# Moving small VectorE operations of the state-space front to GpSimd and ScalarE, and regrouping TensorE's sums and transposes

## The chip, the core and the metric

The kernel runs on one core of a Trainium2 chip, as one program. The metric is the device time of that core in microseconds. The engines work through queues of their own and meet only in semaphores: TensorE (PE) multiplies, VectorE (DVE), ScalarE (ACT) and GpSimd (POOL) work element by element, SyncE (SP) issues the DMAs. In the profile a line such as L1766 is a line of the kernel before.

## What is computed

x is 64 x 64 x 256 (64 sequences of 64 steps, width 256). Two attention layers are added to it, then two state-space layers. The change touches only the state-space layers, and of these only the part ahead of the scan, called the front here:

```python
xr, gate = jnp.split(x @ W_in.T, 2, axis=-1)
xr = xr + t_emb[:, None, :]
xc = silu(causal depthwise conv of width 4 over xr + b_conv)
mu = xc.mean(-1, keepdims=True)
var = xc.var(-1, keepdims=True)
xn = (xc - mu) / jnp.sqrt(var + 1e-05) * ln_g + ln_b
Bm, Cm, dt = jnp.split(xn @ W_xproj.T, 3, axis=-1)
dt = jnp.tanh(dt @ W_dt.T + b_dt) * 0.01
A = -jnp.tanh(A_log)
Ad = 1.0 + dt * A
Bd = Bm * jnp.minimum(jnp.linalg.norm(xn, axis=-1, keepdims=True), 1.0)
# scan over time: h = clip(h * Ad + Bd * xn, -10, 10); y = C h
```

## The kernel before

The 64 sequences are cut into 8 groups of 8, so a group has 512 tokens (columns) and the inner width 512 lies in 4 blocks of 128 partitions. A layer runs a front over the groups, a scan in two passes of four groups, and an output part. The program is written for each engine by hand: every engine has a `body(it, ...)` that lists its work for one group, and the order in that list is the order in its queue. The loop over the groups 0 to 5 and a body for group 6 (`ahead` false) come first; group 7 is spread over the first steps of the scan (`last_group`). Ahead of body 0 a few lines start group 0.

A body of the front works on two groups at once: the second half of the front of group `it`, and the first half of group `it + 1`. The steps, with the lines of the program:

- TensorE makes the X part (`x_in_proj`, L1177) and the gate part (`gate_in`, `gate_half`, L1177 and L1337) into PSUM banks 0 to 3. VectorE adds the condition (`embed`, L1762), ScalarE makes the first tap of the convolution (`tap`, L796), VectorE the other three (`conv`, L1766, twelve of 512 columns), ScalarE the SiLU (`conv_silu`, L801).
- The mean: TensorE sums with columns of ones (`mean`, L1344, tile 128*32). To spread it over all partitions exactly, the row is split in three bf16 parts: `high` (L893), `remain` (VectorE, `mean_rest`, L1899), `middle` (GpSimd, `mean_middle`, L611), `rows3` (VectorE, `mean_rows`, L1904), and TensorE spreads it (`spread_out`, L1350). VectorE subtracts it (`centred`, L1895, four), ScalarE squares (L909, four), TensorE sums the squares (`variance`, L1344).
- The standard deviation: ScalarE takes Ln and Exp (`log_std`, L913 and L915), VectorE makes a Newton step in three operations (`root`, L1607, L1609, L1611) and has `zr`. Then the same split: `high` on GpSimd (L601), `remain` (L1909), `middle` on GpSimd (L606), `rows3` (L1914), spread, and VectorE multiplies (`gained`, L1924, four), ScalarE adds the bias (`shifted`, L919) and squares again (`squared`, L923).
- The small projections: TensorE has `project_part` (L1369, tile 128*32), the product for dt (`decay`, L1382), the norm sums (`norm`, L1344). ScalarE has `decay_tanh`, VectorE `decay` (`am`, L1935), GpSimd 1/`am` in four operations (`over_decay`, L589 to L596, `rc`). VectorE bounds the squared norm (`norm_bound`, L1929), ScalarE takes Ln and Exp (`log_norm`, L940 and L942), VectorE makes a Newton step and a product (`inverse_norm`), multiplies with 1/`am` (`over_decay`, L1950, `mr`), makes `rB` (`scaled_b`, L1955) and the product carried to the next step, `eC` (`carried`, L1959). TensorE folds both (`fold_b`, L1391 and L1393), VectorE splits the result into three bf16 parts (`split_b`, L1970 to L1976, `tvp`).
- The turns: TensorE transposes the normed x (`turned_x`, L1386, tile 128*128), and it is split in three bf16 parts: `xh` on ScalarE (`high_part`, L947), the rest `xr1` on VectorE (`rest`, L1964), `xmi` on ScalarE (`middle_part`, L951), `xlo` on GpSimd (`last_parts`, L584). SP stores them (`store_parts`), and stores `sg` (`store_gate`), the normed x (`store_x`), C and the decay (`store_decay`) and the parts of B (`store_b`, six DMAs) for each group.

ScalarE holds one of two tables at a time, and loads another with `silu_set` and `logarithm_set` (L708, L704), once each in a body.

## Time and profile before

| | |
|---|---|
| median of 3 runs | 1785.19 us (1783.34 to 1785.89) |
| the profiled execution | 1782.5 us, its span 1780.7 us |
| TensorE busy | 1680.3 us, 94% of the span |
| VectorE busy | 1609.2 us, 90% |
| ScalarE busy | 1306.8 us, 73% |
| GpSimd busy | 685.2 us, 38% |
| VectorE, `conv` (L1766) | 192 of 749 ns, 134.6 us |
| TensorE, X and gate products (L1177) | 456 records of 606 ns, 213.6 us |
| GpSimd, `Uw` of the scan (L627) | 256 of 1345 ns, 335.5 us |

The page gives a single profiled execution. Its 40 slices show the attention until slice 12, then for each layer the front in about four slices, the scan, and the output. A timeline lists one engine's instructions in order of time, with neighbours of one line merged (x4 means four); "idle before" is the time in which the engine had nothing to do, and behind the arrow stands who released it. TensorE's matmuls are pipelined, so the differences of their starts say more than their durations. A 512-column product in float32 has two records.

### The profile page before, as it was taken

The page shows a single profiled execution, that of the slowest core. Times are in us where ns is not written, and L with a number is a line of the kernel's source. Part 1 is how long each engine was busy: PE and PEld are TensorE (multiplying, and loading weights), DVE is VectorE, ACT ScalarE, POOL GpSimd, SP SyncE. Part 2 cuts the span into 40 slices and gives each one's busy share as a digit, 9 for nine tenths or more (in the row PEclk, how much of TensorE's full clock was granted, in tenths as well). Part 3 has the DMA queues.
Part 4 walks back from the last instruction along what each step waited for, and adds up shares of the span by engine and source line. Part 5 has one row for each costly group of instructions (what it writes and reads, how often), then busy time and mean ns, then how long its engine had stood idle before and what let it go on. Part 6 is the DMA issues. An engine that isn't in the chain of part 4 may idle for free. (4 is left out here: it accounts for less than half of the span.)

```text
span 1780.7 us, 43798 instructions
## 1 busy us (share of the span) xinstructions
PE 1680.3 (94%) x14852; PEld 750.7 (42%) x14852; DVE 1609.2 (90%) x2492; ACT 1306.8 (73%) x2213; POOL 685.2 (38%) x702
## 2 busy tenths in 40 slices
PE   7999999999999999789999999999998899999998
PEld 3555555555554555332222224445553322222244
DVE  5899999899877999989999997679999999999975
ACT  5655566565646999889999992079998899999910
POOL 0233233323332223557676550012235576756400
PEclk9999999999999999899999999999998999999999
DMA  4000000000002444544545667524446445456678
GB/s 163 2 1 0 1 1 32 2 1 0 1 1 87 172 152 165 192 146 138 183 149 190 226 187 236 190 87 172 174 145 204 141 150 178 145 195 195 188 232 272
DMA packets 126456, 226.85 MB, mean 127 GB/s; under 512 B 35620, under 2 KB 61220, under 8 KB 117540
## 3 DMA queue, kind: packets, MB, share of 16 engines
q1 hardware_dynamic: 125912, 223.51, 38.1%
q10 hardware_dynamic: 432, 1.84, 0.3%
q8 instruction: 71, 1.16, 0.3%
q14 instruction: 41, 0.34, 0.1%
HBM read 141.95 MB, written 83.36 MB: 127 GB/s over the span
## 5 line engine op out<-in xcount | busy, mean ns | idle before, releaser
L1062 ACT ACTIVATE R<-q,Ast 128x512 f32<-128x512 f32 x1016 | 632.9, 709 | 34.4 <-DVE q L2084 32.1
L2084 DVE SCALAR_TENSOR_TENSOR q<-R,PS 128x512 f32<-128x512 f32 x1008 | 610.6, 680 | 9.4 <-ACT R L1062 6.4
L627 POOL TENSOR_TENSOR Uw<-Ub,rowmask 96x512 bf16<-96x512 bf16 x256 | 335.5, 1345 | 144.0 <-PE PS L1509 131.8
L1509 PE MATMUL PS<-xq,Uw 97*128 97x512 bf16 x1024 | 326.6, 391 | 46.8 <-DVE q L2084 37.4
L1526 PE MATMUL PS<-q,Wy 128*32 128x512 f32 x2016 | 280.1, 611 | 0.4 <-DVE q L2084 0.4
L1509 PEld LDWEIGHTS PS<-xq,Uw 97*128 97x128 bf16 x1024 | 84.6, 97 | 363.5 <-DVE q L2084 271.1
L1177 PE MATMUL PS<-X,Win 128*128 (+1 forms) x456 | 213.6, 606 | 0.1
L1078 PE MATMUL PS<-xn,Wl 128*128 128x512 f32 x384 | 188.0, 614 | 0.7 <-DVE xn L1648 0.7
L548 POOL TENSOR_TENSOR ex<-ex,rs 128x1024 f32<-128x1024 f32 x32 | 77.5, 2423 | 203.2 <-DVE rs L1671 203.2
L1766 DVE SCALAR_TENSOR_TENSOR acc<-xp,Wc,acc 128x512 f32<-128x512 f32 x192 | 134.6, 749 | 2.6 <-DVE eC L1888 0.2
L1177 PEld LDWEIGHTS PS<-X,Win 128*128 128x128 f32 x456 | 82.6, 191 | 92.1 <-issue 91.3
L1575 PE MATMUL PS<-yg,Wo 128*128 128x512 f32 x256 | 113.9, 599 | 0.0
L1529 PE MATMUL PS<-xq,By 96*32 96x512 bf16 x1024 | 110.7, 385 | 0.0
L796 ACT ACTIVATE acc<-xp,Ch,Wc 128x512 f32<-128x512 f32 x64 | 51.9, 815 | 74.7 <-DVE xp L1762 74.5
L772 ACT ACTIVATE vTd<-PS 128x1024 f32<-128x1024 f32 x32 | 32.8, 1025 | 94.4 <-PE PS L1078 94.4
L780 ACT ACTIVATE pT<-PS 128x512 f32<-128x512 f32 x128 | 69.3, 593 | 43.4 <-PE PS L1155 43.2
L1078 PEld LDWEIGHTS PS<-xn,Wl 128*128 128x128 f32 x384 | 66.1, 191 | 56.2 <-issue 51.8
L1658 DVE TENSOR_REDUCE mx<-PS 128x32 f32<-128x2048 f32 x32 | 73.2, 2286 | 17.9 <-PE PS L1139 17.8
L541 POOL TENSOR_TENSOR vsc<-vTd,vs_t 128x1024 f32<-128x1024 f32 x16 | 38.3, 2396 | 110.3 <-ACT vTd L772 110.3
L1668 DVE TENSOR_REDUCE sm<-ex 128x32 f32<-128x2048 f32 x32 | 72.9, 2279 | 6.7 <-ACT ex L784 6.7
L1155 PE MATMUL PS<-ident,ex 128*128 128x128 f32 x512 | 69.3, 277 | 6.5 <-DVE ex L1675 4.5
L2122 DVE SCALAR_TENSOR_TENSOR yf<-xnp,Dsk,PS 128x512 f32<-128x512 f32 x64 | 43.6, 743 | 33.2 <-DMA sgp<-sg_d 30.6
(183 smaller groups left out, 2630.9 us busy)
## 6 DMA issues: line engine op xcount, KB each, us to landing
xq<-xpart_d SPq DMA_DIRECT2D x384, 192.0 KB
sg_d<-sg SPq DMA_DIRECT2D x16, 1024.0 KB, 5.2
xn_d<-z SPq DMA_DIRECT2D x16, 1024.0 KB, 3.9
y_d<-ys SPq DMA_DIRECT2D x64, 256.0 KB, 3.9
xnp<-xn_d SPq DMA_DIRECT2D x16, 1024.0 KB, 8.2
sgp<-sg_d SPq DMA_DIRECT2D x16, 1024.0 KB, 11.7
xpart_d<-xh SPq DMA_DIRECT2D x16, 512.0 KB, 2.9
xpart_d<-xmi SPq DMA_DIRECT2D x16, 512.0 KB, 3.7
```

The source lines that it names most:

```text
L548: pl.tensor_tensor(late_half(ex, r), late_half(ex, r), rs[:, r, :].rearrange("p (j e) -> p j e", j=4)[:, :, 4:8] .unsqueeze(3).broadcast_t ...
L627: pl.tensor_tensor(Uw[0:XROWS, h, w, :, :, :], Ub[0:XROWS, w, 0:N, ds(s0, CH)].rearrange("p n t -> p t n").unsqueeze(2).broadcast_to([XROW ...
L1062: act.activation((end if end and (h, t) == (1, CH - 1) else R)[:, w, :], q[:, t % 2, w, :], ACT.Relu, scale=Ast[:, h, w, t:t + 1], bias=CL ...
L1078: mm = pe.matmul(PS[:, bank, :], Wl[l][:, w, c, m * P:(m + 1) * P], rhs[:, c, :], start=(c == 0), stop=(c == HC - 1))
L1177: mm = pe.matmul(PS[:, m % DC, :], Win[:, c, m * P:(m + 1) * P], X[:, ds(g, 1), c, :].rearrange("p a t -> p (a t)"), start=(c == 0), stop= ...
L1509: pe.matmul(PS[:, w, :], Uw[0:KROWS, h, w, t, :, :].rearrange("p b n -> p (b n)"), xq[0:KROWS, hb, w, s8 % XT, :], start=True, stop=True). ...
L1526: pe.matmul(PS[32 * w:32 * w + 32, 4 + h, :], Wy[:, h, w, t * 32:(t + 1) * 32], last[:, w, :] if last else q[:, s8 % 2, w, :], start=(t == ...
L1529: mm = pe.matmul(PS[32 * w:32 * w + 32, 4 + h, :], By[0:XROWS, h, t, w, MID - t * GB:MID + (CH - t) * GB], xq[0:XROWS, hb, w, xt, :], star ...
L1575: mm = pe.matmul(PS[:, 4 + 2 * (g % 2) + m, :], Wo[:, c, m * P:(m + 1) * P], yg[:, g % 2, c, :], start=(c == 0), stop=(c == DC - 1))
L1658: v.tensor_reduce(mx[:, r, :], PS[:, 0:4, :].rearrange("p j (e k) -> p (j e) k", k=S), AX.X, ALU.max).then_inc(max_r, 1)
L1766: v.scalar_tensor_tensor(out=tiled(acc[:, m, :]), in0=xp[:, m, :, j:j + S], scalar=Wc[:, m, j:j + 1], in1=tiled(acc[:, m, :]), op0=ALU.mul ...
L2084: v.scalar_tensor_tensor(out=q[:, s8 % 2, w, :], in0=R[:, w, :], scalar=2 * CLIP, in1=PS[:, w, :], op0=ALU.min, op1=ALU.subtract).then_inc ...
```

## The change

It moves work between engines, and it reorders all four bodies of the front:

- GpSimd takes over from VectorE the Newton step of the inverse norm, its product with the norm and with 1/`am` (`norm_over_decay`, five operations in place of VectorE's three, one and one, in another arrangement), the carried product `eC` (`carried`), and the last operation of `split_b` (`b_low`). From ScalarE it takes the middle parts 0 and 1 (`middle_part`). It gives `mean_middle` to ScalarE. In its body the order is now: middle and low part 0, norm, carried product, middle and low part 1, low parts 2 and 3, `b_low`.
- ScalarE takes `mean_middle` from GpSimd and the first operation of `split_b` from VectorE (`b_high`, the last of its body). `log_norm` is put behind `high_part` 3 and `mean`, and tap 3 ahead of `gate_silu` 1.
- VectorE keeps two operations of `split_b` (`b_rest`). `decay` goes ahead of the last `conv`, `rest` 3 ahead of `mean_rows`, `scaled_b` between `centred` 1 and 2.
- TensorE: the four `turned_x` stand together, and `norm` 0 and 1, and 2 and 3. The spread of the mean goes ahead of X product 2. Half of gate product 0 of the next group is made ahead of `fold_b`, the other half behind the variance; gate product 2 is whole again.
- In body 6 `split_b` stays on VectorE, and middle parts 0 to 3 on ScalarE. A semaphore `xma_r` is new (middle parts by ScalarE), and SP no longer waits for the middle parts, but only for the low ones.

```diff
+                def middle_part(it, k, cast):
+                    pl.wait_ge(xr1_r, it * TT + k + 1 + TT)
+                    alone(pl)
+                    pl.tensor_copy(xmi[:, k, :], xr1[:, k, :]).then_inc(xmi_r, 1)
+                    pl.wait_ge(xmi_r, cast)
+                    pl.tensor_tensor(xlo[:, k, :], xr1[:, k, :], xmi[:, k, :], ALU.subtract).then_inc(xlo_r, 1)
...
+                def norm_over_decay(it):
+                    pl.wait_ge(n2_r, it + 1)
+                    pl.wait_ge(ng_r, it * 2 + 2)
+                    alone(pl)
+                    pl.tensor_tensor(n3[:, :], n2[:, :], mn[:, :], ALU.mult).then_inc(mn_r, 1)
+                    pl.wait_ge(mn_r, it * 3 + 1)
+                    pl.tensor_tensor(n4[:, :], n3[:, :], mn[:, :], ALU.mult).then_inc(mn_r, 1)
+                    pl.wait_ge(rc_r, it * 4 + 4)
+                    pl.tensor_tensor(n3[:, :], n3[:, :], rc[:, :], ALU.mult).then_inc(mm_r, 1)
+                    pl.wait_ge(mn_r, it * 3 + 2)
+                    alone(pl)
+                    pl.tensor_scalar(n4[:, :], n4[:, :], -0.5, 1.5, ALU.mult, ALU.add).then_inc(mn_r, 1)
+                    pl.wait_ge(mm_r, it + 1)
+                    pl.wait_ge(mn_r, it * 3 + 3)
+                    alone(pl)
+                    pl.tensor_tensor(mr[:, :], n4[:, :], n3[:, :], ALU.mult).then_inc(mr_r, 1)
...
+                def b_low(it):
+                    pl.wait_ge(tv_s, it * 4 + 3)
+                    pl.tensor_tensor(tvp[:, 2, :], tvr[:, :], tvp[:, 1, :], ALU.subtract).then_inc(tv_s, 1)
...
                     over_decay(l * G + g)
-                    mean_middle(l * G + g + 1)
-                    last_parts(l * G + g)
+                    parts_free(l * G + g)
+                    middle_part(l * G + g, 0, g * 2 + (l * (2 * G) + 1))
+                    norm_over_decay(l * G + g)
+                    carried(l * G + g)
+                    middle_part(l * G + g, 1, g * 2 + (l * (2 * G) + 2))
+                    low_part(l * G + g, 2, g * 2 + (l * (2 * G) + 1))
+                    low_part(l * G + g, 3, g * 2 + (l * (2 * G) + 2))
+                    b_low(l * G + g)
...
+                def b_high(it):
+                    act.wait_ge(tv_st, it * (TV_STORES * 16) + TV_STORES * 16)
+                    act.wait_ge(tok_mm, it + 1)
+                    act.activation(tvp[:, 0, :], PS[:, 7, 0:P], ACT.Copy).then_inc(tv_s, 1)
...
                     logarithm_set()
-                    log_norm(it)
                     high_part(it, 3, 3)
                     mean(it + 1)
+                    log_norm(it)
+                    mean_middle(it + 1)
                     minus_c(it)
...
                     square(it + 1, 3)
+                    if ahead:
+                        b_high(it)
...
-                    gate_in(it + 1, g + 1, 0)
                     variance(it, 0, 4)
                     variance(it, 1, 4)
                     variance(it, 2, 4)
                     variance(it, 3, 4)
                     x_in_proj(it, g, 3)
+                    gate_half(it + 1, g + 1, 0, 1)
                     gate_in(it + 1, g + 1, 1)
-                    gate_half(it + 1, g + 1, 2, 0)
                     pe.wait_ge(row_r, it * 2 + (2 * AT + 2))
                     spread_out(5, rows3, zb_mm)
-                    gate_half(it + 1, g + 1, 2, 1)
+                    gate_in(it + 1, g + 1, 2)
                     gate_in(it + 1, g + 1, 3)
...
                     turned_x(it, 2)
-                    norm(it, 0)
                     turned_x(it, 3)
                     pe.wait_ge(dts_r, it + 1)
                     project_part(it, 0)
+                    norm(it, 0)
+                    norm(it, 1)
                     decay(it, PS[:, 4, 0:P])
-                    norm(it, 1)
...
                         x_in_proj(it + 1, g + 1, 1)
+                    pe.wait_ge(row_r, it * 2 + (2 * AT + 3))
+                    spread_out(5, rows3, zm_mm)
                     if ahead:
                         x_in_proj(it + 1, g + 1, 2)
-                    pe.wait_ge(row_r, it * 2 + (2 * AT + 3))
-                    spread_out(5, rows3, zm_mm)
+                        gate_half(it + 2, g + 2, 0, 0)
                     fold_b(it)
...
                     conv(it + 1, 1, 3)
+                    decay(it)
                     conv(it + 1, 2, 3)
-                    decay(it)
...
                     rest(it, 2, 2)
-                    inverse_norm(it)
                     mean_rest(it + 1)
-                    over_decay(it)
-                    scaled_b(it)
-                    carried(it)
+                    rest(it, 3, 3)
                     mean_rows(it + 1)
-                    rest(it, 3, 3)
                     centred(it + 1, 0)
                     centred(it + 1, 1)
+                    scaled_b(it)
                     centred(it + 1, 2)
                     centred(it + 1, 3)
                     if ahead:
                         embed(it + 2, g + 2, 1)
-                    if ahead:
                         embed(it + 2, g + 2, 2)
-                    split_b(it)
+                        b_rest(it)
+                    else:
+                        split_b(it)
```

## Rows read from the trace of the kernel before

**Rows 1.** A window: length, busy PE, PEld, DVE, ACT, POOL (instructions), clock, DMA share, GB/s.

```profile
607.30:632.31 25.01, 24.60 (x256) 13.21 (x255) 23.59 (x48) 23.09 (x43) 6.92 (x11) 1.00 0.43 156
```

**Rows 2.** The timeline of VectorE: start, duration, operation, [idle before it].

```profile
607.96 0.29 DVE L1611 SCALAR_TENSOR_TENSOR zr<-zve,zr 128x128 f32<-128x128 f32 x1
...
618.84 2.18 DVE L1766 SCALAR_TENSOR_TENSOR acc<-xp,Wc,acc 128x512 f32<-128x512 f32 x3
...
623.88 0.29 DVE L1607 SCALAR_TENSOR_TENSOR n<-n,mn 128x128 f32<-128x128 f32 x1 [0.20 <-ACT mn L942]
...
625.06 0.34 DVE L1899 SCALAR_TENSOR_TENSOR remain<-high,masks,PS 128x128 f32<-128x128 bf16 x1
...
626.17 0.34 DVE L1904 SCALAR_TENSOR_TENSOR rows<-middle,masks,remain 128x128 bf16<-128x128 bf16 x1
...
627.33 2.48 DVE L1895 TENSOR_TENSOR z<-zs,PS 128x512 f32<-128x512 f32 x4 [0.21 <-PE PS L1350]
...
631.83 0.29 DVE L1976 TENSOR_TENSOR tvp<-tvr,tvp 128x128 bf16<-128x128 f32 x1
```

**Rows 3.** The timeline of ScalarE in the same period.

```profile
621.05 0.63 ACT L801 ACTIVATE zs<-acc 128x512 f32<-128x512 f32 x1
...
621.70 1.28 ACT L704 ACT_TABLE_LOAD   x1
...
623.66 0.58 ACT L947 ACTIVATE xh<-PS 128x512 bf16<-128x512 f32 x1
...
628.05 2.43 ACT L909 ACTIVATE zq<-z 128x512 f32<-128x512 f32 x4 [0.27 <-DVE z L1895]
...
631.55 0.31 ACT L915 ACTIVATE zr<-zlg 128x128 f32<-128x128 f32 x1
```

**Rows 4.** The timeline of TensorE in the same period.

```profile
618.67 0.43 PE L1344 MATMUL PS<-zq,ones_n 128*32 128x128 f32 x8
...
619.07 1.98 PE L1177 MATMUL PS<-X,Win 128*128 x4
...
621.88 0.40 PE L1344 MATMUL PS<-zq,ones_n 128*32 128x128 f32 x8
...
622.10 0.40 PE L1344 MATMUL PS<-zs,ones_d 128*32 128x128 f32 x8
...
626.84 0.39 PE L1350 MATMUL PS<-rows,spread 128*128 128x128 bf16 x4
```

**Rows 5.** The timeline of GpSimd in the same period.

```profile
608.42 0.29 POOL L601 CAST high<-zr 128x128 bf16<-128x128 f32 x1 [2.47 <-DVE zr L1611]
...
622.52 0.30 POOL L594 TENSOR_SCALAR tvr<-tvr 128x128 f32<-128x128 f32 x1 [0.20 <-POOL tvr L591]
...
626.42 4.53 POOL L584 TENSOR_TENSOR xlo<-xr,xmi 128x512 bf16<-128x512 f32 x4 [0.56 <-ACT xmi L951]
```

**Rows 6.** Line 672 by itself: middle part on GpSimd, last group.

```profile
L672 POOL CAST xmi<-xr x8: 606/610/612, 816.0 to 1457.0; 128x512 bf16<-128x512 f32 x8
```

**Rows 7.** Timelines of VectorE and GpSimd in body 6 and behind it.

```profile
708.11 0.75 DVE L1766 SCALAR_TENSOR_TENSOR acc<-xp,Wc,acc 128x512 f32<-128x512 f32 x1
...
708.24 0.77 POOL L601 CAST high<-zr 128x128 bf16<-128x128 f32 x1 [2.25 <-DVE zr L1611]
...
726.71 5.23 POOL L627 TENSOR_TENSOR Uw<-Ub,rowmask 96x512 bf16<-96x512 bf16 x4
...
730.78 1.31 DVE L1976 TENSOR_TENSOR tvp<-tvr,tvp 128x128 bf16<-128x128 f32 x1
```

**Rows 8.** The timeline of ScalarE ahead of body 0.

```profile
556.21 0.37 ACT L913 ACTIVATE zlg<-PS,eps 128x128 f32<-128x128 f32 x1 [1.69 <-PE PS L1344]
```

**Rows 9.** The timeline of SP's queue in one period.

```profile
608.34 5.23 SPq L343 DMA_DIRECT2D bpart_d<-tvp  x6
```

**Rows 10.** The timeline of VectorE: third Newton step of the first and the seventh group.

```profile
557.60 0.29 DVE L1611 SCALAR_TENSOR_TENSOR zr<-zve,zr 128x128 f32<-128x128 f32 x1
...
707.78 0.29 DVE L1611 SCALAR_TENSOR_TENSOR zr<-zve,zr 128x128 f32<-128x128 f32 x1
```

More of the change, by code:

```diff
@@ L576, in _, with parts_free @@
                 pl.memset(words(pass_tables[0][0]), 0.0).then_inc(tab0_zero, 1)
-                def last_parts(it):
+                def parts_free(it):
                     pl.wait_ge(xq_st, it * 48 + 48)
-                    pl.wait_ge(eC_r, it + 1)
                     alone(pl)
-                    for k in range(TT):
-                        pl.wait_ge(xmi_r, it * TT + k + 1)
-                        pl.tensor_tensor(xlo[:, k, :], xr1[:, k, :], xmi[:, k, :], ALU.subtract).then_inc(xlo_r, 1)
+                def middle_part(it, k, cast):
[4 more added lines that the diff above has]
+                    pl.tensor_tensor(xlo[:, k, :], xr1[:, k, :], xmi[:, k, :], ALU.subtract).then_inc(xlo_r, 1)
@@ new lines, in low_part @@
+                def low_part(it, k, cast):
+                    pl.wait_ge(xma_r, cast)
+                    pl.tensor_tensor(xlo[:, k, :], xr1[:, k, :], xmi[:, k, :], ALU.subtract).then_inc(xlo_r, 1)
+                def norm_over_decay(it):
[14 more added lines that the diff above has]
+                    pl.tensor_tensor(mr[:, :], n4[:, :], n3[:, :], ALU.mult).then_inc(mr_r, 1)
@@ new lines, in carried @@
+                def carried(it):
+                    pl.wait_ge(rB_r, it + 1)
+                    pl.tensor_tensor(eC[:, :].rearrange("p (b t) -> p b t", t=S)[:, :, 0:S - 1],
+                                     Cn[:, :].rearrange("p (b t) -> p b t", t=S)[:, :, 0:S - 1],
+                                     rB[:, :].rearrange("p (b t) -> p b t", t=S)[:, :, 1:S], ALU.mult).then_inc(eC_r, 1)
+                def b_low(it):
+                    pl.wait_ge(tv_s, it * 4 + 3)
+                    pl.tensor_tensor(tvp[:, 2, :], tvr[:, :], tvp[:, 1, :], ALU.subtract).then_inc(tv_s, 1)
@@ L604, in std_middle @@
                     pl.wait_ge(rem_r, it * 2 + (2 * AT + 2))
-                    alone(pl)
-                    pl.tensor_copy(middle[:, :], remain[:, :]).then_inc(mid_r, 1)
-                def mean_middle(it):
-                    pl.wait_ge(rem_r, it * 2 + (2 * AT + 1))
                     alone(pl)
@@ L651, in _ @@
                 over_decay(l * G + G - 2)
-                mean_middle(l * G + G - 2 + 1)
+                norm_over_decay(l * G + G - 2)
+                carried(l * G + G - 2)
                 pl.wait_ge(tab_in[0], l * (16 * TABLES) + 16 * TABLES)
@@ L658, in _ @@
                     stage(0, 0, h, True)
-                last_parts(l * G + G - 2)
+                parts_free(l * G + G - 2)
+                for k in range(TT):
+                    low_part(l * G + G - 2, k, l * (2 * G) + 2 * (G - 2) + k + 1)
                 with pl.Fori(1, 4) as c2:
@@ L958, in body @@
                     gate_silu(it + 1, 0)
+                    tap(it + 1, 3)
                     gate_silu(it + 1, 1)
-                    tap(it + 1, 3)
                     shifted(it, 0)
@@ L1429, in body @@
                     norm(it, 2)
+                    norm(it, 3)
                     pe.wait_ge(dtt_r, it + 1)
                     mean(it + 1, 0)
-                    norm(it, 3)
                     mean(it + 1, 1)
@@ L1964, in rest, with b_rest @@
                     v.tensor_tensor(xr1[:, k, :], PS[:, bank, :], xh[:, k, :], ALU.subtract).then_inc(xr1_r, 1)
+                def b_rest(it):
+                    v.wait_ge(tv_s, it * 4 + 1)
+                    v.tensor_tensor(tvr[:, :], PS[:, 7, 0:P], tvp[:, 0, :], ALU.subtract).then_inc(tv_s, 1)
+                    v.wait_ge(tv_s, it * 4 + 2)
+                    v.tensor_copy(tvp[:, 1, :], tvr[:, :]).then_inc(tv_s, 1)
                 def split_b(it):
@@ L1970, in split_b @@
                     v.tensor_copy(tvp[:, 0, :], PS[:, 7, 0:P]).then_inc(tv_s, 1)
-                    v.wait_ge(tv_s, it * 4 + 1)
-                    v.tensor_tensor(tvr[:, :], PS[:, 7, 0:P], tvp[:, 0, :], ALU.subtract).then_inc(tv_s, 1)
-                    v.wait_ge(tv_s, it * 4 + 2)
-                    v.tensor_copy(tvp[:, 1, :], tvr[:, :]).then_inc(tv_s, 1)
+                    b_rest(it)
                     v.wait_ge(tv_s, it * 4 + 3)
@@ L2018, in body @@
                         embed(it + 2, g + 2, 1)
-                    if ahead:
                         embed(it + 2, g + 2, 2)
-                    split_b(it)
+                        b_rest(it)
+                    else:
+                        split_b(it)
                 def last_group(n):
```

11 lines of the change are left out of this document (6 added, 5 removed).

## The prediction

> **What bounds the kernel now.** I read the page's slices first, to see that the two SSM fronts, where the change sits, are stretches in which three engines are nearly full. Then I cut one period of the loop out of the table by windows [rows 1]: in 25.01 us TensorE is busy 24.60, VectorE 23.59, ScalarE 23.09, GpSimd 6.92, and TensorE's clock is granted in full, so it is at 2.4 GHz. Next the timelines of this period, engine by engine. VectorE starts each instruction about 60 ns before the one ahead ends; its only gaps are waits of 0.2 to 0.3 us. So the period is VectorE's own queue, with TensorE and ScalarE one to two microseconds behind it. A gain per group is had only until the next one binds. There are six such periods in each of two layers (bodies 0 to 6), a seventh body that runs into the scan, and a start ahead of body 0.
>
> I count all times from A, the end of the third Newton step of the standard deviation (`zr`): A = 607.96 + 0.29 = 608.25 in this period [rows 2]. The reader is to see that `high`, the spread, `gained` and all that follows hang on A, so one period is the distance from one A to the next.
>
> **VectorE's work.** Taken away: the three Newton steps and the product `mn` (623.88 to 625.06, 1.2 us by starts), `mr` and `eC` 0.3 each like every 128-wide operation beside them, the first of `split_b`'s four operations 0.3 and the last 0.3 to 0.5 [rows 2]: 2.5 us. From 25.0, less these and less the 0.9 of gaps, VectorE alone would need some 21.6 us. Nothing is added to it, only reordered: `decay` comes ahead of the last convolution, so that one ends at A+13.0 instead of A+12.8 (618.84 + 2.18 = 621.02 before). This last convolution is now what VectorE gives to the critical path.
>
> **From the last convolution to the mean's rows.** ScalarE follows at once with the last `conv_silu` (621.05), the table load 0.65 later, and the first operation behind the table 1.3 later [rows 3]: A+14.96. Before, that was `log_norm`, then `high3`, then the mean. Now it is `high3`, then the mean's high part at A+15.44, then `log_norm` (two of 0.31 like the Exp at 631.55), done at A+16.25. VectorE takes the mean's remainder at A+15.8, ScalarE the middle part at A+16.27 (GpSimd before), VectorE `mean_rows` at A+16.7, and the spread starts near A+17.1. Before, it was A+18.6: `mean_rows` at 626.17, and two X products still ahead of the spread on TensorE. With only one X product ahead of it now, TensorE is at the spread before the rows are. So the mean is 1.5 us earlier, and this is the change's gain.
>
> **From the spread to the next A.** `centred` starts 0.5 later (spread 626.84, `centred` 627.33 [rows 2, 4]), the fourth square begins 3.1 behind the first `centred` start (2.5 before, plus `scaled_b` 0.3 and its wait for `mr` 0.3), lasts 0.6, then come `b_high` 0.2, the tap 0.7, Ln 0.4, Exp 0.3 (zr 631.55), Newton 1.07 [rows 2, 3]. In sum A+17.1 + 0.5 + 3.1 + 0.6 + 0.2 + 0.7 + 0.4 + 0.3 + 1.07 = A+24.0, less 0.1 where starts overlap: A+23.9 as long as GpSimd keeps nobody waiting. TensorE's own work, its starts added up without the waits between them, is near 23.2 with 0.5 off for the shapes (below). ScalarE loses two middle parts (1.05) and gains two 128-wide copies (0.35): 22.4. Neither binds.
>
> **Shapes.** A norm sum alone between 128*128 products took 0.40 from start to start (618.67 to 619.07), between sums of its own shape 0.22 (621.88 to 622.10) [rows 4]. Two norm sums and the turns cease to be interrupted: two or three switches of 0.15 to 0.2, 0.5 us of TensorE. I put it at nothing in the sum, since TensorE waits 0.8 us for `mean_rows` in the new order; it would count if TensorE became the bound.
>
> **GpSimd, where the cost is.** Its chain starts with `am`, at A+12.0 on VectorE. `rc` takes 1.9 more with its self-waits (each some 0.2, the row at 622.52 [rows 5]); beside the convolution I add 0.3. Done A+14.7. Then the new middle part, 0.6 by the casts of the last group [rows 6], self-wait 0.2, low part 1.13 to 1.17 (four take 4.53 [rows 5]): A+16.65. Only then comes the norm chain: four TENSOR_TENSOR at 0.46 less overlap, one TENSOR_SCALAR at 0.30, two self-waits, 2.35 us: `mr` at A+19.0. That is when VectorE reaches `scaled_b` (spread 17.3 + 0.5 + two `centred` 1.2), so the tie costs it 0 to 0.3. `eC` ends at A+20.05; TensorE folds at A+20.2, since its X product and half gate last until then. Behind `eC` GpSimd still owes middle part 1 (0.6), its low part (0.2 + 1.15), low parts 2 and 3 (2.3) and `b_low` (0.46): low part 3 ends at A+24.25, `b_low` at A+24.65. Before, GpSimd was through 2.5 us ahead of the next `std_high`. Now it meets it: `std_high` is wanted at A+24.1 and stands behind `b_low` on its queue, and who waits for it is `std_rest`, and behind that all of VectorE.
>
> **What two engines do to each other.** The rows show that some VectorE operations and GpSimd's shut each other out. GpSimd's cast of `zr`, 0.29 in the usual period [rows 5], took 0.77 where the convolution had started just before it, and ended 0.15 after that. VectorE's `tvp` subtract, 0.29 in the loop [rows 2], took 1.31 beside the four `Uw` products and ended with the last of them [rows 7]. In the new order `tvp`'s cast (A+22.1) meets low part 2 (until 23.1), and Newton steps 2 and 3, which read two SBUF tiles each, meet low part 3 and `b_low`. Step 2 can't run before A+24.25, step 3 ends near A+24.8. Also `mean_rows` meets the first norm product: 0.2. The walk gives a new period of 24.8 us. The lower end of this cost is nothing (period 23.9), the upper is that GpSimd and VectorE take turns at `b_low`, the convolution and `std_high`, 0.5 to 0.8 more: 25.3 to 25.6. I take 24.8, because the 1.31 us row is the same kind of operation on the same tile as the one now moved under GpSimd's products.
>
> The Trainium skill has this as a rule (SBUF — State Buffer, Who interferes with whom): a VectorE operation with two SBUF inputs and a GpSimd operation that reads SBUF hold a shared port exclusively, and the second to issue waits for the whole of the first. It speaks against this change. By the rule the period is 24.8 and the time 1781.3; by engine durations alone it would be 23.9 and 1770.5. The 0.77 and 1.31 us rows agree with it. It also says that one SBUF input is free of this, so `centred`, `rest` and Newton step 1 (PSUM and one tile) don't stall.
>
> **Start, tail, stores.** Ahead of body 0 the variance waited for three X products and a gate product, and ScalarE 1.69 us for the variance [rows 8]. Now half a gate product stands there: two matmul records less, of four that took 1.98 with a switch [rows 4], about 0.86 us, in each layer. In the seventh body the spread comes 1.1 us earlier, but `fold_b` and so the variance wait for GpSimd's `eC` (A+20.0, was A+18.6), and the first `Uw` products start 1.5 us later; against that VectorE ends sooner. I put it at +0.3 per layer, bounds -1 and +1. SP's queue: the part stores move 1.5 us back with low part 3, and with them the six `bpart_d` stores (5.23 us of issue [rows 9]), which would then end at A+6.9, 0.8 behind the time when `store_x` wants to go. `centred` needs that store at A+17.6, so it is hidden. `high0` needs the parts landed at A+7.7; they land some 6.5 us after low part 3, about A+6: hidden, with 1.5 us to spare.
>
> **Sum.** From the first A to the seventh, six periods took 150.2 us in layer 0 (`zr` at 557.60 and 707.78 [rows 10]); layer 1 is taken as equal. 6 x 24.8 = 148.8: a gain of 1.4, twice 2.8. Start 2 x 0.86 = 1.7, tail -2 x 0.3 = -0.6. Together 3.9 us. The profiled execution (span 1780.7, time 1782.5) would become 1778.6; it lies 2.7 under the median of the three runs, 1785.19, so I predict 1781.3.
>
> **Rivals.** (1) *GpSimd stays hidden.* Period 23.9, the sum above on the ScalarE and VectorE path: 12 x 0.9 = 10.8 less, 1770.5. For it: 18 us of GpSimd idle in each period. Against it: the order puts 4.6 us of its work behind `eC`, which can't be earlier than A+19.6 as `log_norm` ends at A+16.25. Chance 0.24. (2) *GpSimd becomes the bound.* `std_high` behind `b_low`, `b_low` behind a convolution (0.74), and the self-waits longer than in the `rc` chain. It decides once `b_low` ends more than 0.9 us after the time at which the next `zr` would be ready: period 25.6, 12 x 0.8 = 9.6 more, 1790.9. At 25.2 it is a draw. Against it: the stall needs several collisions to fall the wrong way. Chance 0.20. (3) *The change moves the wait only*: `scaled_b`, now in the middle of `centred`, waits for `mr`, and `b_rest` for ScalarE's `b_high`, a further 0.3: period 25.1, 12 x 0.3 = 3.6 more, 1784.9. Chance 0.14. The forecast's own case, period 24.5 to 25.0, time 1777.7 to 1783.7: 0.42.
>
> **Range and chances.** 8 in 10 from 1769 to 1791, which takes in rivals 1 and 3 and most of rival 2. A measurement of this kernel tells some 0.2% (3.6 us) from no change. Faster by more: rival 1 and rather more than half of the forecast's case (1781.6 is the mark), 0.50. Within: the rest of it, rival 3 and a quarter of rival 2: 0.34. Slower: 0.16.
>
> **What would show it.** Right: `mean_rows` 1.5 us nearer to A; VectorE's `tvp` cast or Newton steps of 0.8 to 1.2 us in place of 0.3; GpSimd with no idle time ahead of `std_high`; ScalarE idle less than 0.5 us before the fourth square. Wrong: Newton steps at 0.29 and GpSimd idle ahead of `std_high` (rival 1); `remain` on VectorE waiting for `high` for over 0.3 us (rival 2); VectorE idle ahead of `scaled_b` (rival 3); a granted clock of TensorE under 1 within the loop, which nothing here provides for.

## The result and the profile after

The changed kernel takes 1774.65 us (median of 4 runs, 1773.23 to 1777.25) against 1785.54 for the kernel before beside it (4 runs): a ratio of 0.9945, interval 0.9929 to 0.996. In a second series on another occasion (`after_again`, below) it was 0.9928 (0.9914 to 0.9941). The change is 10.9 us faster where 3.9 were forecast. The time lies inside the range, and outside the forecast's own case (1777.7 to 1783.7), between it and rival 1.

| profiled execution | before | after |
|---|---|---|
| time, span | 1782.5, 1780.7 us | 1777.3, 1775.4 us |
| TensorE busy | 1680.3 us | 1672.0 us |
| VectorE busy | 1609.2 us | 1596.5 us |
| ScalarE busy | 1306.8 us | 1298.3 us |
| GpSimd busy | 685.2 us | 737.0 us |
| six periods, layer 0 and 1 | 150.2 and 150.7 us | 144.8 and 145.0 us |

One period of the changed kernel by the table of windows (columns as in [rows 1]). The A's, ends of the third Newton step, are at 608.52 and 632.61:

```profile
608.52:632.61 24.09, 23.78 (x256) 13.67 (x255) 22.67 (x40) 22.41 (x43) 10.87 (x19) 1.00 0.44 162
```

Against [rows 1] VectorE has 0.9 us less to do, GpSimd 4.0 more, and the period is 0.9 shorter. TensorE is busy in all but 0.3 of it. VectorE's timeline of this period answers to [rows 2]:

```profile
620.43 0.27 DVE L1983 TENSOR_SCALAR am<-dtt,A 128x128 f32<-128x128 f32 x1
620.62 0.74 DVE L1814 SCALAR_TENSOR_TENSOR acc<-xp,Wc,acc 128x512 f32<-128x512 f32 x1
...
625.00 0.45 DVE L1952 SCALAR_TENSOR_TENSOR rows<-middle,masks,remain 128x128 bf16<-128x128 bf16 x1
626.03 1.29 DVE L1943 TENSOR_TENSOR z<-zs,PS 128x512 f32<-128x512 f32 x2 [0.57 <-PE PS L1397]
627.23 0.28 DVE L2003 TENSOR_TENSOR rB<-PS,mr 128x128 f32<-128x128 f32 x1
...
630.13 0.86 DVE L2018 CAST tvp<-tvr 128x128 bf16<-128x128 f32 x1
630.95 0.29 DVE L1655 SCALAR_TENSOR_TENSOR zve<-PS,zr 128x128 f32<-128x128 f32 x1
631.28 0.90 DVE L1657 SCALAR_TENSOR_TENSOR zve<-zve,zr 128x128 f32<-128x128 f32 x1
632.21 0.40 DVE L1659 SCALAR_TENSOR_TENSOR zr<-zve,zr 128x128 f32<-128x128 f32 x1
```

And GpSimd's, which answers to [rows 5]:

```profile
620.97 0.56 POOL L623 TENSOR_SCALAR rc<-am 128x128 f32<-128x128 f32 x1 [10.72 <-DVE am L1983]
...
622.65 0.46 POOL L630 TENSOR_TENSOR rc<-tvr,rc 128x128 f32<-128x128 f32 x1
623.05 0.61 POOL L585 CAST xmi<-xr 128x512 bf16<-128x512 f32 x1
623.74 1.16 POOL L587 TENSOR_TENSOR xlo<-xr,xmi 128x512 bf16<-128x512 f32 x1
...
626.70 0.46 POOL L608 TENSOR_TENSOR mr<-n 128x128 f32<-128x128 f32 x1 [0.17 <-POOL n L604]
627.59 0.41 POOL L612 TENSOR_TENSOR eC<-Cn,rB 128x126 f32<-128x126 f32 x1 [0.44 <-DVE rB L2003]
...
629.76 2.27 POOL L591 TENSOR_TENSOR xlo<-xr,xmi 128x512 bf16<-128x512 f32 x2
631.99 0.47 POOL L618 TENSOR_TENSOR tvp<-tvr,tvp 128x128 bf16<-128x128 f32 x1
632.78 0.29 POOL L635 CAST high<-zr 128x128 bf16<-128x128 f32 x1 [0.32 <-DVE zr L1659]
```

Laid side by side, the two show the hold-ups. The second Newton step takes 0.90 where one takes 0.29: it ends at 632.18, 0.15 after low part 3 (629.76 + 2.27 = 632.03). The third ends at 632.61, 0.15 after `b_low` (632.46). So A is set by the end of `b_low`, and that by a chain on GpSimd which began with `am`, itself 11.9 us behind the last A: `am`, `rc`, one middle and low part, the norm, `eC`, three low parts, `b_low`, A. The mean's chain joins it at `eC`, which needs `rB`: `mr` is ready at 627.16, and VectorE comes to `rB` at 627.23, behind its second `centred`. So two chains, within 0.1 us of each other, set the end of `b_low`. TensorE's timeline has its only gap, 0.31, where the rows of the deviation are waited for:

```profile
610.71 0.40 PE L1397 MATMUL PS<-rows,spread 128*128 128x128 bf16 x4 [0.31 <-DVE rows L1962]
```

**Outside the periods.** From the first `centred` of a layer to A it was 8.01 and 7.98 us, and is 7.49 and 7.02 (`after_again` 7.03 twice). From the last A to VectorE's first operation on a scan product (`q`) it was 23.94 and 23.92, and is 24.70 and 23.77 (`after_again` 24.54 and 24.19). The two fronts together are 11.9 us shorter in the profiled execution and 12.2 in `after_again`'s. What is left of the kernel is the same code, and it varies from one execution to the next: it took (span less the two fronts) 1416.0 us in this profile of before, 1417.5 in `before_grouped` and between 1411.9 and 1424.2 in the other profiles. In after it was 1422.6, 6.6 more than before, so the two profiled spans differ by only 5.3 although the fronts gave 11.9. Some 3 us of it are one gap, in attention, on TensorE's timeline of after; `newton_in_psum` runs the same matmuls without it (second fence):

```profile
135.67 2.60 PE L1125 MATMUL PS<-av,Wl 128*128 128x512 f32 x4 [2.84 <-issue]
```

```profile
132.16 1.98 PE L1125 MATMUL PS<-av,Wl 128*128 128x512 f32 x4
```

"issue" means that nothing in the profile released the engine. A gap of 2.8 to 3.2 us stands at this place in after, `after_again`, `psum_ungrouped`, `middles_on_scalar` and `spread_late`, and in none of the nine other profiles, that of before among them. Its cause is open. Both profiles of the changed kernel have it, so it may be in its medians too; nothing here separates it from them.

### The profile page after: what moved, and what is told of

Its sections match the earlier page's. It is cut to its first block and busy times, and to the rows that moved or that the text cites. A ratio compares the mean times of both kernels' runs of the same rounds, so it can differ in the third digit from the quotient of the medians.

```text
span 1775.4 us, 43884 instructions
## 1 busy us (share of the span) xinstructions
PE 1672.0 (94%) x14852; PEld 758.4 (43%) x14852; DVE 1596.5 (90%) x2384; ACT 1298.3 (73%) x2215; POOL 737.0 (42%) x808
## 5 line engine op out<-in xcount | busy, mean ns | idle before, releaser
L1224 PE MATMUL PS<-X,Win 128*128 (+1 forms) x456 | 217.2, 609 | 0.1
```

The costliest lines, as they stand in the source:

```text
L1224: mm = pe.matmul(PS[:, m % DC, :], Win[:, c, m * P:(m + 1) * P], X[:, ds(g, 1), c, :].rearrange("p a t -> p (a t)"), start=(c == 0), stop= ...
```

## The experiments

My theory after the result: A follows `b_low` by the hold-up that the prediction described, and the forecast was short only because GpSimd's chain is 0.7 us quicker than I made it. (Some of the expectations call the way in which a VectorE and a GpSimd operation shut each other out "the lock".) The rival: TensorE, busy for 23.78 of 24.09, or VectorE's shorter queue, sets the period, and the long Newton steps cost nothing. All periods below are the mean of the inner ones (second to sixth) of a layer, over both layers. They repeat within 0.04 us, except in the last two runs of this section and in the kernel before and `before_grouped`, where the sixth period is 24.8 and the others are 25.02 in layer 0 and 25.12 in layer 1.

**newton_in_psum.** In the loop the Newton steps keep their temporary in free PSUM columns, so that the second and third read one SBUF tile instead of two.

```diff
-                    root(zr[:, :], PS[:, bank, 0:P], EPS_IN, zr[:, :], zve[:, :], zr_r, it * 3)
+                    tmp = PS[:, 4, P:2 * P] if bank == 4 else zve[:, :]
+                    root(zr[:, :], PS[:, bank, 0:P], EPS_IN, zr[:, :], tmp, zr_r, it * 3)
```

> The changed kernel with one edit: in the front's loop the intermediate result of the Newton step of the standard deviation (zve) lies in PSUM, bank 4, columns 128 to 255, instead of SBUF. So steps 2 and 3 read one SBUF tile each, not two. Theory P (the two engines shut each other out, and GpSimd's low parts hold up the Newton steps): step 2 falls from 0.90 to 0.3 us, step 3 from 0.40 to 0.3, zr is ready 0.7 us sooner, but the cast of zr on GpSimd still stands behind b_low, so of this 0.3 is left: period 23.8 instead of 24.1, 3 to 4 us less in all. Rival Q (GpSimd's queue alone sets the pace, and VectorE only waits for it): steps may shorten, the period stays 24.1. Rival T (TensorE is already the bound): period 24.1 too, and TensorE's idle time ahead of the spread of the deviation, 0.3 now, grows elsewhere.

Measured: 1765.0 us (6 runs, 1762.11 to 1770.4), ratio to before 0.9898 (0.9883 to 0.9913); period 23.70, as theory P had it to 0.1. VectorE's timeline, and below it GpSimd's and TensorE's:

```profile
600.60 0.86 DVE L2019 CAST tvp<-tvr 128x128 bf16<-128x128 f32 x1
601.42 0.30 DVE L1655 SCALAR_TENSOR_TENSOR PS<-PS,zr 128x128 f32<-128x128 f32 x1
601.75 0.30 DVE L1657 SCALAR_TENSOR_TENSOR PS<-PS,zr 128x128 f32<-128x128 f32 x1
602.09 0.29 DVE L1659 SCALAR_TENSOR_TENSOR zr<-PS,zr 128x128 f32<-128x128 f32 x1
602.52 0.91 DVE L1814 SCALAR_TENSOR_TENSOR acc<-xp,Wc,acc 128x512 f32<-128x512 f32 x1
```

```profile
600.23 2.27 POOL L591 TENSOR_TENSOR xlo<-xr,xmi 128x512 bf16<-128x512 f32 x2
602.45 0.43 POOL L618 TENSOR_TENSOR tvp<-tvr,tvp 128x128 bf16<-128x128 f32 x1
602.82 0.75 POOL L635 CAST high<-zr 128x128 bf16<-128x128 f32 x1
```

```profile
595.98 0.40 PE L1397 MATMUL PS<-rows,spread 128*128 128x128 bf16 x4
...
603.07 1.88 PE L1224 MATMUL PS<-X,Win 128*128 x4
604.88 0.40 PE L1397 MATMUL PS<-rows,spread 128*128 128x128 bf16 x4
```

GpSimd's low part 3 runs until 602.50, and the second Newton step, in the midst of it, takes 0.30. So the 0.90 was the shared access, not the operation. The edit moves the result of step 2 to PSUM as well as an input; step 3 tells the two apart, for it still writes `zr` in SBUF, reads one SBUF tile, and takes 0.29 at 602.09, also beside low part 3, where with two SBUF tiles it took 1.12 beside one (`low3_twice`, below). The Trainium skill has it so (SBUF — State Buffer, Who interferes with whom): a VectorE operation with two SBUF inputs contends with a GpSimd operation that reads SBUF, and one with at most one SBUF input doesn't, unless it runs in a two-port mode, which the page says a cast can do. The trace agrees on the Newton steps, 0.90 and 0.30; and the `tvp` cast, with one SBUF input, is held up, 0.86 where it takes 0.23 in the kernel before. TensorE now goes from product to spread without a gap, and the period is TensorE's. The hold-up moved on: the convolution takes 0.91 and `high` 0.75. This version beats both kernels: its interval ends at 0.9913, that of the unchanged one in the same series begins at 0.9914.

**after_again.** The changed kernel unaltered, beside it.

> The changed kernel itself, beside the others on one chip. Time 1773 to 1776 us, 10 to 12 less than before. The gap of 3.1 us in TensorE's instruction supply that the profile of the changed kernel has at 134 us, in an attention body that the change doesn't touch: if it belongs to the one execution, it is absent here; if to the code's place in memory, it is here again. Tail of layer 0: the first scan product waits for a DMA again, 1 to 2 us.

Measured: 1771.1 us (6 runs, 1766.72 to 1772.84), 2 below the expected 1773, period 24.09 again. The gap in attention is there again (2.98 us), and so are the waits of the scan for the parts (1.96 and 1.35). Between this median and that of `newton_in_psum` lie 6.1 us; the two fronts of their profiled executions differ by 4.0 (twice 2.6 from the first `centred` to the last A, less 0.5 and 0.7 in the tails). So 4.0 is what the edit is seen to do. The gap, which `newton_in_psum` doesn't have, may account for the rest.

**low3_zeroed and low3_twice.** GpSimd's last low part of groups 0 to 5 replaced by a fill with zeros (this leaves that part of the split out), or computed twice.

```diff
-                    low_part(l * G + g, 3, g * 2 + (l * (2 * G) + 2))
+                    pl.memset(xlo[:, 3, :], 0.0).then_inc(xlo_r, 1)
```

```diff
+                    pl.tensor_tensor(apart[:, 0, :], xr1[:, 3, :], xmi[:, 3, :], ALU.subtract).then_inc(ap_r, 1)
                     low_part(l * G + g, 3, g * 2 + (l * (2 * G) + 2))
```

> The changed kernel with low part 3 left out in groups 0 to 5 (GpSimd writes zeros there without reading SBUF, some 0.3 us instead of 1.16). GpSimd is through 0.9 us sooner. Theory P: Newton step 2 falls from 0.90 to 0.3 to 0.5, period 23.8, where TensorE, whose only idle time in the period is 0.3, becomes the bound. Rival T: period stays 24.1. Forecast of the record (GpSimd's queue worth 0.7 per 0.7): 23.4.

> The changed kernel with low part 3 computed twice in groups 0 to 5 (the first time into a tile that nobody reads), so 1.13 us more of GpSimd ahead of the next cast of zr. Theory P and rival Q: period 24.1 + 1.1 = 25.2, 13 us more in all. Rival T (TensorE the bound, GpSimd hidden): 24.1 to 24.4, 0 to 3 us more.

Measured: 23.72 and 24.98 us a period (23.8 and 25.2 expected). Taking 0.6 away gains 0.37, as far as TensorE's floor of 23.7; adding 1.11 costs 0.89. So the end of GpSimd's queue sets the period from TensorE's floor upwards. VectorE's timeline of `low3_twice`:

```profile
629.96 0.91 DVE L1663 SCALAR_TENSOR_TENSOR zve<-zve,zr 128x128 f32<-128x128 f32 x1
630.90 1.12 DVE L1665 SCALAR_TENSOR_TENSOR zr<-zve,zr 128x128 f32<-128x128 f32 x1
...
633.10 0.35 DVE L1963 SCALAR_TENSOR_TENSOR remain<-high,masks,zr 128x128 f32<-128x128 bf16 x1 [0.18 <-POOL high L636]
```

Each Newton step waits for one whole low part. The third gets ahead of `b_low`, so that A no longer waits for its 0.43; in return `high`, behind `b_low` and the convolution, takes 0.81, and `remain` waits 0.18 for it. This is how 1.11 comes to cost only 0.89.

**psum_low3_twice.** Both edits at once.

> newton_in_psum (period 23.70 us) with the fourth low part computed twice on GpSimd, 1.11 us more, the first copy into a buffer that nobody reads. In low3_twice, where the Newton steps keep their temporary in SBUF, the same addition cost 0.88 us. Theory A (the only link from GpSimd to VectorE at that place is the lock, and it is gone from two of the three Newton steps): the next link is GpSimd's own order, since the high part of the next deviation stands behind the low parts; GpSimd's chain then ends at about 25.0 from the end of the Newton step, and the period becomes 24.5 to 24.9. Theory B (GpSimd has that much slack without the lock): 23.7 to 23.9. What lies between tells how much slack GpSimd has once the lock is gone.

Measured: 24.80, within theory A. I had written that the next link would be GpSimd's order alone. The rows show order and hold-up together: VectorE's convolution, then GpSimd's `b_low` (behind which stands `high`), then TensorE:

```profile
628.47 1.64 DVE L1820 SCALAR_TENSOR_TENSOR acc<-xp,Wc,acc 128x512 f32<-128x512 f32 x1
```

```profile
629.52 0.87 POOL L619 TENSOR_TENSOR tvp<-tvr,tvp 128x128 bf16<-128x128 f32 x1
```

```profile
631.93 0.40 PE L1403 MATMUL PS<-rows,spread 128*128 128x128 bf16 x4 [1.02 <-DVE rows L1968]
```

The convolution waits 0.8 for the low part, then `b_low` 0.4 for the convolution, and TensorE 1.0 for the rows behind both. Of 1.11 added, 1.09 shows: `newton_in_psum` has no slack left on GpSimd either. This is the order of collisions of rival 2 of the prediction (`remain` waits 0.55 for `high`), at a load that the changed kernel doesn't have.

**The grouping by shape: before_grouped, shapes_ungrouped, psum_ungrouped.** TensorE's order alone, put into the kernel before, taken out of the changed one, and taken out of `newton_in_psum` (the cut shows it taken out).

```diff
                     turned_x(it, 2)
+                    norm(it, 0)
                     turned_x(it, 3)
                     pe.wait_ge(dts_r, it + 1)
                     project_part(it, 0)
-                    norm(it, 0)
-                    norm(it, 1)
                     decay(it, PS[:, 4, 0:P])
+                    norm(it, 1)
...
                     norm(it, 2)
-                    norm(it, 3)
                     pe.wait_ge(dtt_r, it + 1)
                     mean(it + 1, 0)
+                    norm(it, 3)
```

> The kernel before with only TensorE's grouping by tile shape added, and nothing of the moves to GpSimd and ScalarE. Theory (the kernel before is bound by VectorE and its waits, at 25.03 us a period, and TensorE has about 1.3 us of idle time in it): the period stays within 0.1 us of 25.03; TensorE's busy time falls by 0.3 to 0.5 and its idle time grows by as much. Rival (TensorE's own order brings the gain): the period falls to 24.5 to 24.7.

> The changed kernel with one part undone: TensorE's norm sums and turns stand in the order of the kernel before (norm sum 0 between turns 2 and 3, the decay matmul between norm sums 0 and 1, the mean of block 0 between norm sums 2 and 3). In the changed kernel TensorE is busy 23.78 us of the 24.09 us period and idle 0.30 us, ahead of the spread of the deviation. Theory (TensorE close to the bound, and each change of tile shape costs it something): the prediction priced the switches at 0.5 us together; 0.3 of it goes into the idle time, so the period becomes 24.2 to 24.4 us and that idle time disappears. Rival (a change of shape costs nothing that lasts): 24.09 us with the idle time as it is. A second rival: the order matters by when the norm and the mean are ready and not by TensorE's own time; then the spread of the mean would wait longer than before while the busy time stays 23.8.

> newton_in_psum (period 23.70 us, no idle time of TensorE left in it) with the norm sums and turns in the order of the kernel before. Here TensorE alone sets the period, so the price of the shape changes is read directly. Theory: 0.5 us for the changes together, period 24.2. If each costs only its share of pipeline fill, 23.9. Rival (they cost nothing): 23.70.

One window of each, in this order:

```profile
605.10:630.10 25.00, 24.19 (x256) 13.34 (x255) 23.59 (x49) 23.05 (x43) 6.90 (x11) 1.00 0.43 156
```

```profile
604.70:629.03 24.33, 24.02 (x256) 13.54 (x254) 22.65 (x40) 22.56 (x43) 10.90 (x20) 1.00 0.44 160
```

```profile
609.36:633.32 23.96, 23.96 (x256) 13.54 (x255) 22.08 (x41) 22.58 (x43) 11.29 (x20) 1.00 0.45 163
```

In the kernel before the grouping takes 0.41 off TensorE's busy time [rows 1] and nothing off the period: TensorE's own work is not the bound there. That VectorE's queue is, remains the prediction's reading of the timelines; no run shortens that queue alone. Taken out of the changed kernel, it adds 0.24 to the busy time and 0.24 to the period; its 0.3 of idle time stays. With TensorE alone in charge it is 0.26 (period 23.97). So the switches cost half of the 0.5 I put on them, and in the changed kernel they count. The theory's figure for `shapes_ungrouped`, 24.2 to 24.4, was met but its way was not: TensorE's idle time took up none of it. VectorE's timeline there has a wait of 0.49 for the X product that now comes later, and GpSimd's norm chain one of 0.19 for `mn`, so that the other chain is moved by as much:

```profile
618.46 0.69 DVE L1810 TENSOR_TENSOR xp<-PS,cond 128x512 f32<-128x512 f32 x1 [0.49 <-PE PS L1224]
```

**lognorm_first.** ScalarE's two norm operations ahead of `high3` and the mean.

```diff
+                    log_norm(it)
                     high_part(it, 3, 3)
                     mean(it + 1)
-                    log_norm(it)
```

> The changed kernel with ScalarE's two norm operations (0.31 us each, 0.5 us in a row) ahead of the last rounding to the high part (0.60) and of the high part of the mean (0.27). This gives GpSimd's norm chain its input 1.0 us sooner, and the mean's rows 0.5 us later. Theory (two chains of nearly one length share the period: the mean's rows to the Newton steps, and GpSimd's norm chain to the low parts, whose lock delays the same Newton steps): the chain of the mean is the one that TensorE waits on, so the period grows, to 24.4 to 24.6 us. Rival (GpSimd's chain alone sets the period): its low parts end up to 1.0 us sooner, the Newton steps are not held up, and the period falls to 23.7 to 23.8.

Measured: 24.61, the theory's figure. The norm chain of GpSimd does not start sooner, as low part 0 ends only then; `eC` waits 0.92 us for `rB`, which stands behind `centred` on VectorE, and the mean's rows are 0.5 later. It pays that the change has the mean first.

**spread_late.** The spread of the mean behind one more X product.

```diff
                     if ahead:
                         x_in_proj(it + 1, g + 1, 1)
+                    if ahead:
+                        x_in_proj(it + 1, g + 1, 2)
                     pe.wait_ge(row_r, it * 2 + (2 * AT + 3))
                     spread_out(5, rows3, zm_mm)
-                        x_in_proj(it + 1, g + 1, 2)
```

> The changed kernel with TensorE's spread of the mean put behind the third X product of the next group (1.98 us), with nothing else changed. It asks whether the chain from the mean's rows (ready at 625.45, TensorE takes them at 625.51) through centring, squares and Newton steps to the next spread is the one that closes the period together with TensorE. Theory: centring starts 2.0 us later, and so do squares, variance and the end of the Newton steps; the lock's hold-ups on them (1.2) go, because the low parts end first: period 24.7 to 25.6 us, likeliest 25.2. Rival (TensorE alone is the bound, and the chain has slack): within 0.2 of 24.09.

Measured: 25.67, a little over the range: 1.58 for 1.98 of delay. The Newton steps are still held up (0.94 and 0.40), because GpSimd's `eC` waits for `rB` and so its low parts move back with the mean; I had left this link out. VectorE's timeline shows the start of centring:

```profile
629.55 1.28 DVE L1944 TENSOR_TENSOR z<-zs,PS 128x512 f32<-128x512 f32 x2 [2.16 <-PE PS L1397]
```

**norm_on_vector.** Root of the norm, `mr` and `eC` back on VectorE at their old places.

```diff
                     rest(it, 2, 2)
+                    inverse_norm(it)
                     mean_rest(it + 1)
+                    over_decay(it)
                     rest(it, 3, 3)
...
                     scaled_b(it)
+                    carried(it)
```

> The changed kernel with one part undone: the root of the norm, the product with the decay (mr) and the carried product (eC) run on VectorE again, each at the place in VectorE's order that it had in the kernel before; the other moves and TensorE's grouping stay. VectorE takes back seven instructions of 0.32 to 0.33 us from start to start (1.3 for the root, 0.3 for mr, 0.2 for eC), all ahead of the mean's last subtraction or between it and the Newton steps; GpSimd gives up 2.8 us. Theory (VectorE's queue ahead of the mean's rows sets when TensorE can spread the mean): the rows end 1.3 to 2.0 us later from the end of the Newton step, GpSimd's low parts end before the Newton steps, so that 0.6 to 1.2 us of the hold-ups goes: period 24.3 to 25.2 us, likeliest 24.7, against 24.09. Rival (what was gained is TensorE's grouping and rounding on GpSimd, not this move): 24.1 or below.

Measured: 27.6 to 28.2 (1813.81 us), far over the 25.2 expected. VectorE's and GpSimd's timelines:

```profile
628.40 0.29 DVE L1651 SCALAR_TENSOR_TENSOR n<-n,mn 128x128 f32<-128x128 f32 x1 [1.04 <-ACT mn L976]
628.72 0.58 DVE L1653 SCALAR_TENSOR_TENSOR n<-n,mn 128x128 f32<-128x128 f32 x1
629.34 1.20 DVE L1655 SCALAR_TENSOR_TENSOR mn<-n,mn 128x128 f32<-128x128 f32 x1
...
634.26 1.09 DVE L2003 TENSOR_TENSOR eC<-Cn,rB 128x126 f32<-128x126 f32 x1
```

```profile
628.48 0.68 POOL L585 CAST xmi<-xr 128x512 bf16<-128x512 f32 x1
629.24 1.15 POOL L587 TENSOR_TENSOR xlo<-xr,xmi 128x512 bf16<-128x512 f32 x1
632.93 2.28 POOL L591 TENSOR_TENSOR xlo<-xr,xmi 128x512 bf16<-128x512 f32 x2 [2.54 <-ACT xmi L985]
```

The root meets GpSimd's middle and low part 1, which with the norm gone come this early: its steps take 0.58 and 1.20, `eC` beside low parts 2 and 3 1.09, 2.0 us of hold-ups where I had counted none, and 1.04 of waiting for `mn`, which ScalarE gives later than in the kernel before as the mean goes first. The mean's rows end 20.1 us behind A instead of 16.9. The two lengths of the period differ by the granted clock (last section). So this undo prices not seven instructions but a collision that neither kernel has; what the move of the norm is worth by itself stays open.

**middles_on_scalar.** Middle parts 0 and 1 back on ScalarE; GpSimd's low part 0 keeps its place ahead of the norm.

```diff
-                    middle_part(l * G + g, 0, g * 2 + (l * (2 * G) + 1))
+                    low_part(l * G + g, 0, g * 4 + (l * 28 + 1))
                     norm_over_decay(l * G + g)
```

> The changed kernel with one part undone: middle parts 0 and 1 are rounded by ScalarE as in the kernel before, so that GpSimd gives up two casts of 0.61 us and ScalarE takes 1.14 us more in a row ahead of the squares. Theory (TensorE 23.7 is the floor; beside it GpSimd's end decides, by the lock, and ScalarE's squares decide, by the variance): GpSimd's low parts end about 1.2 us sooner and free the second Newton step (-0.6), while the squares and with them the variance come up to 1.1 us later: period 24.1 to 24.6 us, likeliest 24.3. Rival (ScalarE has slack for them): 23.7 to 23.8. Second rival (ScalarE was a bound of its own, 22.4 busy of 24.1): 25.0.

Measured: 25.97 in some periods, 27.30 in others (1809.53 us). GpSimd's timeline, and VectorE's:

```profile
631.90 1.16 POOL L591 TENSOR_TENSOR xlo<-xr,xmi 128x512 bf16<-128x512 f32 x1 [3.20 <-ACT xmi L989]
```

```profile
635.34 0.29 DVE L2002 TENSOR_TENSOR rB<-PS,mr 128x128 f32<-128x128 f32 x1 [2.55 <-POOL mr L608]
```

GpSimd's queue stands 3.2 us at low part 0, which needs ScalarE's first middle part, and the norm stands behind it. I had asked only how busy the two engines are, not what is first in a queue. Three windows of it:

```profile
667.00:694.00 27.00, 25.34 (x254) 14.39 (x254) 21.32 (x40) 23.19 (x45) 9.38 (x17) 0.94 0.46 160
666.00:667.00 1.00, 1.00 (x2) 0.48 (x2) 0.40 (x2) 0.95 (x3) 1.00 (x2) 0.50 0.00 0
1222.70:1248.70 26.00, 24.30 (x255) 13.63 (x254) 21.51 (x41) 23.23 (x45) 9.80 (x17) 1.00 0.41 150
```

TensorE stands still for 1.7 us ahead of `fold_b` in both. In the periods of 27.3 its granted clock is 0.94 in the mean: behind the gap it falls from 1.00 to 0.50, the lower level, 1.2 GHz (middle row), and what lies from `fold_b` to the end of the next X product takes 5.4 us (663.00 to 668.42) instead of 4.0 (1244.30 to 1248.33). In the period 1222.7 to 1248.7 it is 1.00 throughout. That is another 1.3 a period on top of the wait.

## Why the prediction was right, and where it was off

The time fell inside a range 22 us wide, and the gain was 2.8 times the one forecast. The mechanism that the forecast rests on is there; its lengths were too long, that of TensorE's own work excepted, which was too short.

**The bound of before** was right in what could be tried: `before_grouped` took 0.41 us of TensorE's work away and left the period alone. What each single move is worth stays open, as both undos of a move brought waits that neither kernel has. That the earlier mean counts is shown from the other side: its rows 0.5 later cost 0.52 a period (`lognorm_first`), its spread 1.98 later 1.58 (`spread_late`).

**From the last convolution to the spread** was right to 0.2: the convolution ends at A+12.84 (A+13.0), `mean_rows` starts at A+16.5 (A+16.7; before, A+17.9), the spread at A+16.99 (A+17.1). The mean is 1.4 us nearer to A.

**The hold-ups** were right in kind and place: the `tvp` cast 0.86, the second Newton step 0.90, `mean_rows` 0.45 instead of 0.34. That A would follow `b_low` by 0.15 came from [rows 7] and is what happens (632.46 to 632.61).

**From the spread to A, were nobody held up,** was mis-sized by 0.4 and never came to show. I added up 6.8 us (A+17.1 to A+23.9). `newton_in_psum` needs 6.4, from the spread at 595.98 to A at 602.38: the fourth square starts 2.7 behind `centred`, not 3.1, as `rB` waits for nothing. From A+16.99 this would give a period of 23.4, below TensorE's own 23.7.

**GpSimd's chain is the term that was mis-sized**, and it carries the whole step from 24.8 to 24.09 (end times):

| offset from A | predicted | measured |
|---|---|---|
| `rc` done | 14.7 | 14.6 |
| low part 0 done | 16.65 | 16.4 |
| `mr` done | 19.0 | 18.6 |
| `eC` done | 20.05 | 19.5 |
| low part 3 done | 24.25 | 23.5 |
| `b_low` done | 24.65 | 23.94 |

No link is wrong by more than 0.2. I added a self-wait (GpSimd waiting for its own last result) of 0.2 between a cast and its low part, where the starts are 0.69 apart for a cast of 0.61; and I let `rB` and `eC` wait for each other a little longer than they do (0.44). There the mean's chain has its share: this walk took the spread at A+17.3, where the one before it had 17.1 and it measured 16.99, so `rB` starts at A+18.7 instead of 19.0. Rounding up along a chain of seventeen instructions gave 0.7, and 0.7 twelve times is 8.5 us, more than the gain forecast.

**TensorE's own work** I put at 23.2, "neither binds". It is 23.7 without any idle time (`newton_in_psum`), and 23.97 without the grouping. So the shapes count for 0.24, not for nothing, and rival 1's 23.9 was nearly the floor, by luck: it was the sum from the ScalarE and VectorE path, which is 23.4, and the floor is TensorE's, which I had at 23.2. An error of 0.5 here would have hidden a real bound, had GpSimd been any quicker.

**Start and tail** were right: -0.86 against a mean of -0.85 over the four layers profiled, and +0.3 against +0.37. In the tail of layer 0 TensorE waits 1.86 us for the part store's load (`xq<-xpart_d`), an end that I hadn't named. SP's queue was right: the six `bpart_d` issues end at A+6.9, hidden.

**Sum.** With the measured lengths it reads -11.1 for the periods, -1.5 for the starts and +0.6 for the tails, 11.9 in place of 3.9; the medians say 10.9 and 12.3.

**Rivals.** Rival 1 was named for idle time on GpSimd ahead of `std_high` and Newton steps of 0.29. The second Newton step takes 0.90, and of the idle time, 2.47 before, 0.32 is left; rival 1's time was nearer all the same. Rival 2's sign, `remain` waiting over 0.3 for `high`, needs 1.1 us more on GpSimd and the Newton steps free of hold-ups (`psum_low3_twice`, 0.55; in `low3_twice` it is 0.18). Rival 3 didn't occur: `rB` follows `centred` without a gap.

## What to carry to other kernels

When work moves to an engine with room, walk its queue as one chain from the operation that starts it to the first wait on it elsewhere, with start-to-start distances from the trace and no safety added at the links; the sum of small margins was larger here than the gain. Where two engines read the same memory at once, ask which operand could lie in PSUM: one such line was worth 0.4 us in each period of 24.1 with no work taken away. And price a partial undo by what now stands first in each queue; both undos here failed by waits that no count of busy time shows.

## What the runs showed that I had not expected

A fill with zeros (0.52 us) held up VectorE like a read: in `low3_zeroed` the `tvp` cast took 1.32 us and ended 0.1 after the fill, which began before it had ended. The operation held up is the cast, with one SBUF input; no run puts a fill beside an operation with two. VectorE's timeline, then GpSimd's:

```profile
624.34 1.32 DVE L2020 CAST tvp<-tvr 128x128 bf16<-128x128 f32 x1
```

```profile
625.06 0.52 POOL L684 MEMSET xlo<- 128x512 bf16 x1
```

A turn can pass from engine to engine: the convolution of `psum_low3_twice` waits for a low part, then holds up `b_low`.

The granted clock fell in some periods and not in others of the same kernel, with the same gap. In `middles_on_scalar` the gap is 1.67 us both where the clock stays at 1.00 and where it falls to 0.50 behind it. In `norm_on_vector` it is 3.05 in each period; in those of 27.6 the clock is 1.00, and in those of 28.2 it falls to 0.50 (690 to 691) and is 0.94 in the mean. The table of windows for one of each:

```profile
639.66:667.24 27.58, 24.34 (x255) 13.83 (x254) 24.91 (x46) 22.51 (x43) 8.55 (x13) 1.00 0.39 141
667.24:695.48 28.24, 25.19 (x255) 14.30 (x254) 25.00 (x46) 22.72 (x43) 8.55 (x13) 0.94 0.41 144
```

So the length of a gap alone doesn't tell, and what does is open.
